# A post-norm attention and expert layer on one core: three waits moved at once

## The chip, the core and the metric

One core of one Trainium2 chip runs the whole layer as one program. Its engines are TensorE (PE, matmuls, with PEld for its weight loads), VectorE (DVE), ScalarE (ACT), GpSimd (POOL) and SyncE (SP, which issues most DMAs). The metric is the device time of one execution in microseconds; the figure compared is the median of several executions.

## The reference, cut to what matters

```
x = layernorm(x + attention(x))        # 4 x 512 tokens, 512 wide, 16 heads of 32
x = layernorm(x + top1_expert_ffn(x))  # 4 experts, 512 -> 2048 -> 512

attention: q, k, v = x @ W + b, split into heads
  s = q k^T / sqrt(32) - slope[head] * (T - 1 - key)     # a bias by key position
  s = where(key <= query, s, -huge);  out = softmax(s) v;  return out @ Wo + bo
ffn: logits = x @ Wr + br, the best expert of each token, silu(x Wg) * (x Wu) @ Wd, times its probability
```

All is fp32. The kernel splits operands into a rounded high part and a low part and adds three products (high*high, low*high, high*low) for each fp32 product.

## The kernel before

The program has two stages. The first is attention over 4 batches of 16 heads; the second gathers the rows of each expert and runs the feed-forward part. The change lies in the first stage alone.

**Steps.** Attention is a pipeline of steps. A head has three units (n = 0, 1, 2: some of its query or key tiles), so 64 heads give units 0 to 191, and step u does the following for units of different age. TensorE runs `unit_scores(u)` (queries by keys), `unit_turned(u - 7)` (the same scores with keys on the partitions), once a head `row_of_maxima` (turning the row maxima), then a slice of side work, `unit_values(u - 10)` (weights by values), once a head `head_values`, and a second slice of side work. VectorE runs `unit_biased(u)` (adds the bias to the scores in place and takes the minimum of the negated sum: the row maximum, line 1290) and `unit_masked(u - 7)` (adds the causal mask to the turned scores, line 1307). ScalarE then runs `unit_exp(u - 7)` (line 1035), and `unit_split` (the high part of the weights) a step later; GpSimd makes the low part one step behind (`unit_low`, line 1627).

**End of a head.** When a head's last unit of values is done, ScalarE copies the sum out of its PSUM bank at the end of its step (`head_copied`, line 1048, tile pvT, in steps with u = 0 modulo 3, behind `unit_exp` of that step). TensorE turns that copy in the next step (`head_values`, line 837, four transposes, u = 1 modulo 3), waiting on the semaphore s_pvT. ScalarE and VectorE read the turned result one step later (lines 1055, 1315, 1316), GpSimd scales it (line 1621).

**Side work.** The projections (jobs K, Q, V of a group of four heads, 12 matmuls of 512 columns or 24 of 256), the transposes of x, the output projection OP with its transposes OT, the layernormed row's transposes x1t and the gate's logits are cut into single matmuls. A planner (`make_plan`) lays them into two halves of each step, `plan.slices[u, 0]` ahead of the values and `plan.slices[u, 1]` behind them, by a queue, a budget for each half step and due times. A finished job is taken over at the start of the next step by ScalarE (high part, `take`) and then VectorE (low part, `take`), both ahead of their units. When the queue is empty, or no job in it is ready, a step has no side work. The plan can be worked out from the code alone: steps 12 to 20 (group 1) hold V for the second half of the first batch's keys, then K and Q of group 2, and steps 21 to 23 hold nothing.

**Order on an engine.** Each engine works strictly in the order in which the code issues. In step u VectorE's order is: take-overs, layernorm moments, layernorm, `unit_biased(u)`, `unit_masked(u - 7)`, `head_values`.

**The stacks.** The scores of a head need its q and k parts laid below each other on 96 partitions (tile stack, six slots). DMAs issued by SyncE put them there. For the first four heads this happens right after the first K and Q: heads 0 and 1 first K, then Q, then heads 2 and 3, six small DMAs for a head (line 563). Later heads get three DMAs each (line 579). ScalarE may overwrite q and k with the next group's K only when all stacks of the group before have landed (line 991 and the waits above it).

Of the kernel before, what the change touches and what calls it, by code (L numbers as in the profile page):

```python
# [110 lines left out]
def is_head_step(u, lag):  # L111

    return u >= lag and (u - lag) % PER_HEAD == 0 and (u - lag) // PER_HEAD < NB * NH
# [50 lines left out]
def make_plan():  # L164
# [76 lines left out]
    for u in range(STEPS):  # L241
        flush(u)
        if u in SPLIT_BY:
            ready.add(("split", SPLIT_BY[u]))
        if later:
            kind, t = later.popleft()
            if kind == "moments":
                plan.moments_at[u] = t
            else:
                plan.normal_at[u] = t  # L250
                fresh.append(("ln", t))
        for t in range(2 * QT, NT):
            if plan.flushed.get(("OP", t - 2 * QT), STEPS) + X_LOAD <= u:
                ready.add(("x", t // QT, t % QT))
        if u < WORK:
            g = min(u // PER_GROUP, NG - 1)
            step = u - g * PER_GROUP
            b, m = divmod(g, GPB)
            if step == 0:

                if g == 0:
                    queue.extend([("K", 1), ("Q", 1), ("bv_wo", 0)])
                elif m == 0:
                    queue.appendleft(("V", g // 2, 1))
                    rows_due.extend((b - 1, n) for n in range(QT + 3))
                elif g == 1:
                    queue.append(("V", 1, 0))
                elif m == 1 or g == 2:
                    queue.appendleft(("V", b * GPB // 2 + 1, 1))
                for _ in range(row_counts[b == LAST][m] if b else 0):  # L270
                    queue.extend(row_jobs(*rows_due.popleft()))
                if m == GPB - 1 and b + 1 < NB:
                    next_x = b + 1
                    queue.append(("V", (g + 1) // 2, 0))
            for j in range(QT):

                if next_x and ("x", next_x, j) in ready and ("xT", next_x, j) not in turned:
                    turned.append(("xT", next_x, j))
                    queue.appendleft(turned[-1])
            if m == 0 and g and step == VL:  # L280
                queue.append(("V", g // 2 + 1, 0))
            if step == KQ_STEP and 0 < g < NG - 1:
                if m == 2 and 0 < b < LAST:
                    queue.extend([("K", g + 1), ("Q", g + 1)])
                else:
                    first = [j for j in queue if j[0] == "xT" or m == 0 and j[0] == "V"]
                    for j in first:
                        queue.remove(j)
                    queue.extendleft(reversed(first + [("K", g + 1), ("Q", g + 1)]))
            if u == U:  # L290
                for t in range(T0, NT):
                    if t > T0:
                        queue.append(("OP", t - 1))
                    queue.append(("OT", t))
                queue.append(("OP", NT - 1))
            work(u, 0, budget(u, 0))
        if is_head_step(u, VL + PER_HEAD + 2):
            ready.add(("o", (u - VL - PER_HEAD - 2) // PER_HEAD))

        if u >= U:  # L300
            ready.update(fresh)
        if u < WORK:
            work(u, 1, budget(u, 1))
        ready.update(fresh)
        fresh.clear()
# [18 lines left out]
def build(nc, x, Wq, bq, Wk, bk, Wv, bv, Wo, bo, Wr, br, Wg, Wu, Wd,  # L324
# [7 lines left out]
    with ExitStack() as ctx:  # L332
# [178 lines left out]
        kqv_done = max(done("K", NG - 1), done("Q", NG - 1), done("V", NG // 2 - 1, 1))  # L511

        def stack_count(hd):
            return 16 * (3 * (hd // NSTK + 1) + (3 if hd % NSTK < GH else 0))

        def x1T_at(t):
            return t % 2 if t >= T0 else 0
# [24 lines left out]
        hot_f = hot_pad[:, NT - 1:2 * NT - 1, :].bitcast(F32)  # L542
        ends, begins, count = route[:, TILES, 0, :], route[:, TILES, 1, :], route[:, TMP, 0, :]
        number, found = banks[2][:, 0:NS], route[:, POS, :, :].rearrange("p t e -> p (t e)")[:, 0:NS]


        def sync(sp):
# [18 lines left out]
            def load_first_stack(h, n, job):  # L566
                sp.wait_ge(s_side_act, plan.act_number[job])
                load_first_part(h, n, False)
                sp.wait_ge(s_side_dve, plan.number[job])
                load_first_part(h, n, True)  # L570

            def load_stacks(hd):

                g, h = divmod(hd, GH)
                sp.wait_ge(s_side_dve, max(done("K", g), done("Q", g)))
                if hd >= NSTK:
                    sp.wait_ge(s_sT, (hd - NSTK + 1) * PER_HEAD)
                for r, (q_part, k_part) in enumerate(STACKED):
                    sp.dma_start(stack[r * HD:(r + 1) * HD, hd % NSTK, :, :].bitcast(F32),
                                 qk[h * HD:(h + 1) * HD, q_part:k_part + 1:k_part - q_part, :].bitcast(F32)  # L580
                                 ).then_inc(s_stack[hd % NSTK], 16)

            def load_row(hd):

# [47 lines left out]
            for h in (0, 1):  # L632
                load_first_stack(h, WK, ("K", 0))
            for h in (0, 1):
                load_first_stack(h, WQ, ("Q", 0))
            for h in (2, 3):
                load_first_stack(h, WK, ("K", 0))
                load_first_stack(h, WQ, ("Q", 0))
            next_stack = GH
            for u in range(STEPS):  # L640
# [36 lines left out]
        def tensor(pe):  # L677
# [155 lines left out]
            def head_values(hd):  # L833
                bank = banks[4 + hd % 2]
                pe.wait_ge(s_pvT, hd + 1)
                for i in range(QT):
                    mm = pe.transpose(bank[:, i * VW:(i + 1) * VW], pvT[:, i * P:(i + 1) * P], ident[0:VW, 0:VW])
                mm.then_inc(s_back, 1)
# [3 lines left out]
            for u in range(STEPS):  # L842
                if u < U:
                    unit_scores(u)
                if LAG <= u < U + LAG:
                    unit_turned(u - LAG)
                if is_head_step(u, ROW_AT):
                    row_of_maxima((u - ROW_AT) // PER_HEAD)
                if u < WORK:
                    for job, i0, i1 in plan.slices[u, 0]:  # L850
                        side(job, i0, i1)
                if u >= VL:
                    unit_values(u - VL)
                if is_head_step(u, VL + PER_HEAD):
                    head_values((u - VL - PER_HEAD) // PER_HEAD)
                if u < WORK:
                    for job, i0, i1 in plan.slices[u, 1]:
                        side(job, i0, i1)
            head_values(NB * NH - 1)
            for job in plan.after_loop + plan.tail:  # L860
                side(job, 0, len(cost_of(job)))
# [100 lines left out]
        def scalar(act):  # L962
            def split_weight(n, part):
                cols = columns(n, part)
                if n == WQ:
                    act.wait_ge(s_wq, part + 1)
                else:
                    act.wait_ge(s_w[n, part], 16)
                act.activation(w_hi[n][:, :, cols], w_raw[:, n, :, cols], ACT.Copy).then_inc(s_whi, 1)
# [110 lines left out]
            take(("Q", 0))  # L1080
            split_weight(WK, 1)
            split_weight(WQ, 1)
            take(("V", 0, 0))
            take(("V", 0, 1))
            split_weight(WV, 1)
# [128 lines left out]
        def vector(dve):  # L1214
# [61 lines left out]
            def normalise(t):  # L1276
                dve.wait_ge(s_rstd, t + 1)
                dve.tensor_scalar(x1_row(t), x1_row(t), mv[:, t % 2, 0:1], rstd[:, t % 2, 1:2],
                                  ALU.subtract, ALU.mult).then_inc(s_ln, 1)
# [30 lines left out]
            def head_values(hd):  # L1310
                parts = banks[4 + hd % 2][:, 0:QT * VW].rearrange("p (i d) -> p i d", i=QT)
                dve.wait_ge(s_pvhi, hd + 1)
                if hd >= 2:
                    dve.wait_ge(s_o, hd - 1)
                dve.reciprocal(row_inv[:, hd % 2, :], pv_hi[:, hd % 2, :, HD]).then_inc(s_inv, 1)
                dve.tensor_tensor(pv_sum[:, hd % 2, :, :], parts[:, :, HD + 1:VW], pv_hi[:, hd % 2, :, 0:HD],
                                  ALU.add).then_inc(s_pvsum, 1)
# [11 lines left out]
            for u in range(STEPS):  # L1329
                for job in plan.taken_at[u]:  # L1330
                    take(job)
                if u in plan.moments_at:
                    moments(plan.moments_at[u])
                if u in plan.normal_at:
                    normalise(plan.normal_at[u])
                if u < U:
                    unit_biased(u)
                if LAG <= u < U + LAG:
                    unit_masked(u - LAG)
                if is_head_step(u, VL + PER_HEAD + 1):  # L1340
                    head_values((u - VL - PER_HEAD - 1) // PER_HEAD)
            head_values(NB * NH - 1)
# [426 lines left out]
```

## Time and profile before

| | before |
|---|---|
| median of 2 executions | 1288.54 us (1288.02 to 1289.06) |
| profiled execution: time, span | 1292.03 us, 1290.2 us |
| TensorE busy over the span | 1169.2 us (91%) |
| VectorE, ScalarE, GpSimd busy | 729.2 us (57%), 588.6 us (46%), 521.6 us (40%) |
| granted TensorE clock, mean | 0.947 of full |

Every number below is from the one profiled execution. A span runs from the first instruction to the last. The granted clock is a share of 2.4 GHz: 1.00 is the full level and 0.50 the lower one of 1.2 GHz. In the timeline the bracket at the end of a row is the time for which the engine stood idle before it and what ended that. The attention stage runs from the start to about 530 us, the feed-forward stage from about 565 us.

### The profile page before, as it was taken

The numbers are of one execution on the slowest core, as the hardware profiler recorded it, in microseconds if no ns is written. First come the engines' busy times: TensorE is split into PE (matmuls) and PEld (weight loads), VectorE is DVE, ScalarE is ACT, GpSimd is POOL, SyncE is SP. The second block draws the span as 40 slices with busy tenths as digits, with TensorE's granted clock in tenths as the row PEclk, the third lists the DMA queues.
The fourth block names the chain that finished last, engine by engine and source line by source line (L and its number), as shares of the span: only waits on it lengthen the run. The fifth ranks groups of instructions, "written<-read, shape, count | busy, mean of one in ns | idle before, by whom it ended". The sixth has DMA issues, their size and how long they took to land.

```text
span 1290.2 us, 25813 instructions
## 1 busy us (share of the span) xinstructions
PE 1169.2 (91%) x7658; PEld 1040.4 (81%) x7658; DVE 729.2 (57%) x1975; ACT 588.6 (46%) x1475; POOL 521.6 (40%) x662
## 2 busy tenths in 40 slices
PE   7888888998898888669999999999999999999994
PEld 5677777777787676559988998899889988998993
DVE  4555556556655564456565456645664566366565
ACT  3577765676576557424232323332333233233344
POOL 6855644565455456453133123302330232033236
PEclk9898998999889887769999999999999999999997
DMA  8223323222322232144212231223122313231302
GB/s 271 56 50 71 67 74 84 58 62 65 88 55 58 58 77 63 51 124 129 83 58 74 72 94 53 80 66 99 50 83 67 99 50 83 67 99 42 91 26 106
DMA packets 105534, 100.10 MB, mean 78 GB/s; under 512 B 10367, under 2 KB 79615, under 8 KB 105408
## 3 DMA queue, kind: packets, MB, share of 16 engines
q1 hardware_dynamic: 100640, 87.97, 25.4%
q0 software_dynamic: 3040, 9.18, 2.2%
q8 instruction: 75, 1.23, 0.4%
q10 hardware_dynamic: 1728, 1.31, 0.3%
q14 instruction: 51, 0.42, 0.1%
HBM read 64.74 MB, written 9.18 MB: 57 GB/s over the span
## 4 chain that ended last, share of the span: by engine, by line
PE 48%; POOL 6%; DMA 3%; issue 3%; ACT 2%; DVE 2%; SPq 0%; ACTq 0%; POOLq 0%; DVEq 0%
PE bank L910 34%; PE bank L935 8%; POOL up_lo L1636 5%; PE bank L922 2%; DMA up_raw<-in_Wu_dram 2%; PE bank L682 1%; ACT up_hi L1065 1%; PE bank L776 1%; PE bank L884 1%; POOL out_dram L1703 1%; ACT probs L1035 0%; DVE bank L1290 0%; DMA y<-x_scratch,row_token 0%; PE bank L828 0%; PE bank L872 0%
## 5 line engine op out<-in xcount | busy, mean ns | idle before, releaser
L1636 POOL TENSOR_TENSOR up_lo<-up_raw,up_hi 128x256 fp32r<-128x256 f32 x241 | 171.6, 747 | 480.8 <-ACT up_hi L1065 480.6
L910 PE MATMUL bank<-up_hi,xsT_hi 128*128 x1216 | 356.2, 293 | 8.4 <-POOL up_lo L1636 6.6
L910 PE MATMUL bank<-up_hi,xsT_lo 128*128 x1216 | 344.6, 283 | 0.0
L910 PE MATMUL bank<-up_lo,xsT_hi 128*128 x1216 | 344.5, 283 | 0.0
L1627 POOL TENSOR_TENSOR pT_lo<-probs,pT_hi 128x512 fp32r<-128x512 f32 (+1 forms) x192 | 210.7, 1103 | 188.4 <-ACT pT_hi L1042 187.8
L1451 DVE SCALAR_TENSOR_TENSOR h_tok<-bank,row_weight,silu 128x128 f32<-128x128 f32 x304 | 93.4, 347 | 294.7 <-ACT silu L1145 294.7
L910 PEld LDWEIGHTS bank<-up_hi,xsT_hi 128*128 128x128 f32 x1216 | 233.3, 192 | 15.1 <-issue 14.9
L910 PEld LDWEIGHTS bank<-up_hi,xsT_lo 128*128 128x128 f32 x1216 | 234.0, 192 | 0.3
L910 PEld LDWEIGHTS bank<-up_lo,xsT_hi 128*128 128x128 f32 x1216 | 233.6, 192 | 0.0
L1145 ACT ACTIVATE silu<-bank 128x256 f32<-128x256 f32 (+1 forms) x160 | 59.9, 374 | 367.5 <-PE bank L910 367.5
L1468 DVE TENSOR_TENSOR y<-bank,y 128x512 f32<-128x512 f32 x295 | 199.0, 689 | 0.5
L1035 ACT ACTIVATE probs<-bank,key_bias 128x256 f32<-128x256 f32 (+3 forms) x256 | 126.4, 519 | 109.0 <-DVE bank L1307 109.0
L1290 DVE CUSTOM_DVE_ANT_0 bank<-bank,dist 128x512 f32<-128x512 f32 (+3 forms) x256 | 123.2, 503 | 78.5 <-PE bank L788 78.0
L935 PE MATMUL bank<-down_hi,hT_hi 128*128 x304 | 124.2, 408 | 1.3 <-DVE y L1468 0.6
L1065 ACT ACTIVATE up_hi<-up_raw 128x256 fp32r<-128x256 f32 x256 | 85.3, 408 | 83.5 <-DMA up_raw<-in_Wu_dram 83.5
L935 PE MATMUL bank<-down_lo,hT_hi 128*128 x304 | 119.1, 392 | 0.0
L935 PE MATMUL bank<-down_hi,hT_lo 128*128 x304 | 119.0, 392 | 0.0
L1042 ACT ACTIVATE pT_hi<-probs 128x512 fp32r<-128x512 f32 (+1 forms) x192 | 106.8, 556 | 2.3
L828 PE MATMUL bank<-pT_hi,v 128*65 128x256 f32 (+2 forms) x320 | 86.0, 303 | 1.6 <-POOL pT_lo L1627 1.6
L788 PE MATMUL bank<-stack 96*128 96x512 f32 (+3 forms) x256 | 82.7, 365 | 4.3 <-DVE neg_max L1290 4.1
L828 PE MATMUL bank<-pT_lo,v 128*65 128x256 f32 (+3 forms) x256 | 76.7, 325 | 0.0
L803 PE MATMUL bank<-stack 97*128 97x256 f32 (+3 forms) x256 | 74.6, 333 | 1.1 <-ACT probs L1035 0.9
(181 smaller groups left out, 2096.8 us busy)
## 6 DMA issues: line engine op xcount, KB each, us to landing
stack<-qk SPq DMA_DIRECT2D x180, 128.0 KB, 2.4
up_raw<-in_Wg_dram SPq DMA_DIRECT2D x64, 256.0 KB, 3.1
up_raw<-in_Wu_dram SPq DMA_DIRECT2D x64, 256.0 KB, 3.8
down_raw<-in_Wd_dram SPq DMA_DIRECT2D x64, 256.0 KB, 2.6
x_tok<-in_x_dram SPq DMA_DIRECT2D x16, 256.0 KB, 4.4
x_scratch<-res SPq DMA_DIRECT2D x12, 256.0 KB, 2.2
stack<-qk SPq DMA_DIRECT2D x24, 64.0 KB, 3.2
w_raw<-in_Wo_dram SPq DMA_DIRECT2D x1, 1024.0 KB, 8.8
```

The costliest lines, as they stand in the source:

```text
L788: mm = pe.matmul(bank[:, at:at + width], q_stack[0:3 * HD, slot, i * P:(i + 1) * P], k_stack[0:3 * HD, slot, 0:width], start=True, stop=True)
L828: mm = pe.matmul(bank[0:VW, c0:c1], v[:, g // 2 % 2, j, g % 2 * GH + h, :], part[:, u % NP, at + c0 - j * P:at + c1 - j * P], start=(j == ...
L910: mm = pe.matmul(bank[:, n * 2 * P:(n + 1) * 2 * P], a[:, s, k, :], up_w[w][k][:, :, :].rearrange("p a f -> p (a f)")[:, bass.ds(at, 2 * P ...
L935: mm = pe.matmul(bank[:, :], a[:, s, :], down_w[w][:, :, :].rearrange("p a f -> p (a f)")[:, bass.ds(at, D)], start=(q == 0), stop=(q == 2))
L1035: ex = act.activation(probs[:, u % NP, at:at + width], banks[2 + u % 2][:, at:at + width], ACT.Exp, scale=SLOPE[hd % NH], bias=key_bias[:, ...
L1042: act.activation(pT_hi[:, u % NP, 0:n], probs[:, u % NP, 0:n], ACT.Copy).then_inc(s_pThi, 1)
L1065: act.activation(up_w[0][k][:, e, :], up_raw[:, idx % NUPS, k, :, :].rearrange("p g f -> p (g f)"), ACT.Copy).then_inc(s_uphi, 1)
L1290: bi = dve.tensor_tensor_reduce(out=banks[u % 2][:, at:at + width], in0=banks[u % 2][:, at:at + width], in1=dist[:, SEQ - width:SEQ], scal ...
L1451: hh = dve.scalar_tensor_tensor(h_tok[:, idx % 2, n, :], gu[:, n, 1, :], row_weight[:, s:s + 1], silu[:, idx % 2, n, :], ALU.mult, ALU.mult)
L1468: dve.tensor_tensor(y[:, s, :], banks[D_BANKS[idx % 3]][:, :], y[:, s, :], ALU.add).then_inc(s_y, 1)
L1627: pool.tensor_tensor(pT_lo[:, u % NP, 0:n], probs[:, u % NP, 0:n], pT_hi[:, u % NP, 0:n].bitcast(F32), ALU.subtract).then_inc(s_pTlo, 1)
L1636: pool.tensor_tensor(up_w[1][k][:, e, :], up_raw[:, idx % NUPS, k, :, :].rearrange("p g f -> p (g f)"), up_w[0][k][:, e, :].bitcast(F32), ...
```

## The change

Four edits, all in the attention stage.

1. TensorE issues `head_values` as the last thing of its step, behind the second slice of side work, not ahead of it.
2. VectorE issues `unit_masked(u - 7)` ahead of `unit_biased(u)`.
3. The stacks of heads 2 and 3 are issued by ScalarE, three whole DMAs for each head, after the first K and Q are through VectorE; SyncE issues those of heads 0 and 1 only. The counts waited for follow.
4. In group 1 (steps 12 to 23) the planner queues the job V of the next two groups behind K and Q, at the third step; before, it was queued at the first step and ran ahead of them.

```
-                elif g == 1:
-                    queue.append(("V", 1, 0))
-                elif m == 1 or g == 2:
+                elif m == 1 and b or g == 2:
                     queue.appendleft(("V", b * GPB // 2 + 1, 1))
...
             if step == KQ_STEP and 0 < g < NG - 1:
-                if m == 2 and 0 < b < LAST:
+                if g == 1:
+                    queue.extend([("K", 2), ("Q", 2), ("V", 1, 0)])
+                elif m == 2 and 0 < b < LAST:
...
-            return 16 * (3 * (hd // NSTK + 1) + (3 if hd % NSTK < GH else 0))
+            return 16 * (3 * (hd // NSTK + 1) + (3 if hd % NSTK < GH // 2 else 0))
...
             for h in (0, 1):
-                load_first_stack(h, WQ, ("Q", 0))
-            for h in (2, 3):
-                load_first_stack(h, WK, ("K", 0))
                 load_first_stack(h, WQ, ("Q", 0))
...
                 if u >= VL:
                     unit_values(u - VL)
-                if is_head_step(u, VL + PER_HEAD):
-                    head_values((u - VL - PER_HEAD) // PER_HEAD)
                 if u < WORK:
                     for job, i0, i1 in plan.slices[u, 1]:
                         side(job, i0, i1)
+                if is_head_step(u, VL + PER_HEAD):
+                    head_values((u - VL - PER_HEAD) // PER_HEAD)
...
             split_weight(WQ, 1)
+            act.wait_ge(s_side_dve, done("Q", 0))
+            for h in (2, 3):
+                for r, (q_part, k_part) in enumerate(STACKED):
+                    act.dma_start(stack[r * HD:(r + 1) * HD, h, :, :].bitcast(F32),
+                                  stack_rows(h, q_part, k_part)).then_inc(s_stack[h], 16)
             take(("V", 0, 0))
...
+                if LAG <= u < U + LAG:
+                    unit_masked(u - LAG)
                 if u < U:
                     unit_biased(u)
-                if LAG <= u < U + LAG:
-                    unit_masked(u - LAG)
```

## Rows read from the trace of the kernel before

**Rows 1.** Waits of TensorE over the span: engine, line, releaser: us, times, longest

```profile
PE bank L837 <- ACT pvT L1048: 42.6, 38, 2.8
```

**Rows 2.** Timeline of steps 100 to 103: start us, us, engine, line, operation

```profile
264.85 0.46 PE L837 MATMUL bank<-ident,pvT 65*128 65x65 f32 x4 [0.64 <-ACT pvT L1048]
...
266.07 0.40 PE L682 MATMUL bank<-xT_lo,w_hi 128*128 128x512 f32 x1
...
266.31 0.39 PE L682 MATMUL bank<-xT_hi,w_hi 128*128 128x512 f32 x1
...
267.68 0.69 ACT L991 ACTIVATE qk<-bank,bias_col 128x512 fp32r<-128x512 f32 x1
...
268.40 0.75 DVE L1235 SCALAR_TENSOR_TENSOR qk<-bank,bias_col,qk 128x512 fp32r<-128x512 f32 x1 [1.29 <-ACT qk L991]
...
269.06 0.69 DVE L1290 CUSTOM_DVE_ANT_0 bank<-bank,dist 128x512 f32<-128x512 f32 x1
...
269.67 0.47 DVE L1307 TENSOR_TENSOR bank<-bank,causal 128x256 f32<-128x256 f32 x1
...
270.17 0.84 ACT L1035 ACTIVATE probs<-bank,key_bias 128x384 f32<-128x384 f32 x2 [1.29 <-DVE bank L1307]
...
270.90 0.59 ACT L1048 ACTIVATE pvT<-bank 65x512 f32<-65x512 f32 x1
...
271.54 0.46 PE L837 MATMUL bank<-ident,pvT 65*128 65x65 f32 x4 [0.77 <-ACT pvT L1048]
271.81 0.48 PE L682 MATMUL bank<-xT_hi,w_hi 128*128 128x512 f32 x1
```

**Rows 3.** Timeline of TensorE, line 837, two heads with side work

```profile
59.20 0.46 PE L837 MATMUL bank<-ident,pvT 65*128 65x65 f32 x4 [0.61 <-ACT pvT L1048]
...
432.25 0.46 PE L837 MATMUL bank<-ident,pvT 65*128 65x65 f32 x4 [0.88 <-ACT pvT L1048]
```

**Rows 4.** Timeline of TensorE, line 837, a head with a V job beside it

```profile
152.87 0.46 PE L837 MATMUL bank<-ident,pvT 65*128 65x65 f32 x4 [1.52 <-ACT pvT L1048]
```

**Rows 5.** Timeline of TensorE, line 837, heads beside the output projection, and one more wait

```profile
192.55 0.46 PE L837 MATMUL bank<-ident,pvT 65*128 65x65 f32 x4 [1.79 <-ACT pvT L1048]
...
201.75 0.46 PE L837 MATMUL bank<-ident,pvT 65*128 65x65 f32 x4 [1.17 <-ACT pvT L1048]
...
202.96 0.50 PE L682 MATMUL bank<-xT_hi,w_hi 128*128 128x512 f32 x1 [0.30 <-DVE oT_lo L1247]
```

**Rows 6.** Timeline of TensorE, line 837, heads without side work

```profile
72.56 0.46 PE L837 MATMUL bank<-ident,pvT 65*128 65x65 f32 x4 [2.21 <-ACT pvT L1048]
...
346.47 0.46 PE L837 MATMUL bank<-ident,pvT 65*128 65x65 f32 x4 [2.83 <-ACT pvT L1048]
```

**Rows 7.** Timeline of TensorE, line 837, the last head

```profile
523.11 0.47 PE L837 MATMUL bank<-ident,pvT 65*128 65x65 f32 x4 [0.68 <-ACT pvT L1048]
```

**Rows 8.** Busy us in two stretches: stretch, length, PE, PEld, DVE, ACT, POOL, PEclk, DMA, GB/s

```profile
266.00:273.00 7.00, 6.23 (x37) 4.97 (x36) 3.89 (x15) 5.21 (x13) 3.94 (x5) 1.00 0.00 0
...
75.00:77.50 2.50, 2.50 (x13) 2.31 (x13) 0.62 (x3) 2.30 (x5) 1.73 (x3) 0.50 0.51 116
```

**Rows 9.** Timeline of the start, engine by engine (SPq is a DMA issue)

```profile
17.63 16.31 SPq L563 DMA_DIRECT2D stack<-qk  x24
...
20.22 2.85 ACT L969 ACTIVATE w_hi<-w_raw 128x1536 fp32r<-128x1536 f32 x2
24.46 0.61 ACT L996 ACTIVATE v<-bank 128x512 fp32r<-128x512 f32 x1 [1.39 <-PE bank L682]
...
35.46 0.69 ACT L991 ACTIVATE qk<-bank,bias_col 128x512 fp32r<-128x512 f32 x1 [6.57 <-DMA stack<-qk]
...
37.72 0.76 PE L788 MATMUL bank<-stack 96*128 96x512 f32 x1 [3.43 <-DVE neg_max L1290]
...
39.23 0.30 POOL L1585 TENSOR_SCALAR causal<-causal 128x128 f32<-128x128 f32 x1
...
41.64 0.77 PE L788 MATMUL bank<-stack 96*128 96x512 f32 x1 [0.70 <-DVE neg_max L1290]
```

More of the change, by code:

```diff
@@ L544, in build, with stack_rows @@
         number, found = banks[2][:, 0:NS], route[:, POS, :, :].rearrange("p t e -> p (t e)")[:, 0:NS]
+        def stack_rows(h, q_part, k_part):
+            return qk[h * HD:(h + 1) * HD, q_part:k_part + 1:k_part - q_part, :].bitcast(F32)
         def sync(sp):
@@ L579, in load_stacks @@
                     sp.dma_start(stack[r * HD:(r + 1) * HD, hd % NSTK, :, :].bitcast(F32),
-                                 qk[h * HD:(h + 1) * HD, q_part:k_part + 1:k_part - q_part, :].bitcast(F32)
-                                 ).then_inc(s_stack[hd % NSTK], 16)
+                                 stack_rows(h, q_part, k_part)).then_inc(s_stack[hd % NSTK], 16)
             def load_row(hd):
```

## The prediction, made before the change was run

> **What bounds the kernel now.** I read the waits of TensorE first, since it is busy for 91% of the span and whatever it waits for is lost. One line leads the list by far: the four transposes that turn a head's values wait 42.6 us, in 38 of the 64 heads, for ScalarE's copy of these values [rows 1]. I then followed that wait through the timeline of every head, to see which chain is late and what TensorE could have done meanwhile. Last came the start and the windows of the granted clock. The feed-forward stage is untouched and only starts earlier.
>
> One head shows the chain [rows 2]. At step 102 ScalarE takes over a finished Q at 267.68, VectorE its low part at 268.40, then VectorE takes the minimum of step 102 from 269.06, then adds the mask at 269.67; the exponential follows at 270.17, the copy behind it at 270.90, and TensorE, already in step 103, goes on at 271.54 after 0.77 us of idle time. The matmuls right behind the transposes (271.81) are side work that needs none of this. So the wait holds up work that was ready, and the chain that ends it carries a minimum that nobody on the chain needs.
>
> **Edit 1, the transposes behind the second slice.** TensorE now does that slice while the copy is made. Two matmuls of 512 columns are the usual slice; they start 0.24 us apart at the full clock (266.07 and 266.31 [rows 2]), so it hides 0.48 us; three hide 0.72 us, and so do six V matmuls of 256 columns, at half the price each. What is queued behind the transposes is the next step's scores; who waits for them is ScalarE, one step later, ahead of its exponential. That exponential waits for turned scores of that later step in any case, which TensorE issues behind these transposes, so I cost the later arrival at nothing. If ScalarE were not about a step behind, it would cost up to the slice, 0.48 us a head.
>
> **Edit 2, the mask first.** The mask moves up by the spacing of the two VectorE instructions, 269.67 - 269.06 = 0.61 us, and so do the exponential and the copy [rows 2]. VectorE now waits for the turned scores before it takes the minimum: the minimum ends about as late as the mask is long, 0.47 us, plus the wait for one more group of matmuls where VectorE is early. Behind it hang the scores two steps on. The minimum would end at 269.06 + 0.47 + 0.69 = 270.2, 2.5 us after the take-over at 267.68, near the start of its step; a head takes 271.54 - 264.85 = 6.7 us now [rows 2], about 6.0 without the wait, and two of its three steps 4.0 us. So more than a microsecond is to spare, and I cost it at nothing; the third rival is the case that this is wrong.
>
> **The 38 waits, by what lies beside them.** They add up as follows, each read from its own row of the timeline, with the plan of side work beside it.
> - 18 heads with an ordinary slice in the second half, 0.16 to 0.88 us, 10.9 us together (the first and last: 0.61 and 0.88) [rows 3]. Slice and mask give 0.48 + 0.61 = 1.09 us, more than any of them. Gain 10.9 us.
> - 3 heads with six V matmuls in both halves, 1.52, 1.51 and 1.51 us, of which one stands [rows 4]. 0.72 + 0.61 = 1.33, and the slice of the first half also runs ahead of the wait. I take 1.4 each: 4.2 us.
> - 4 heads beside the output projection, 1.79, 1.80, 1.97 and 2.57 us (the first stands [rows 5]). Three matmuls and the mask: 0.72 + 0.61 = 1.3 each, 5.2 us.
> - 2 heads with a transpose and K matmuls in the second half, 1.17 and 1.16 us. Here the slice itself waits on VectorE, 0.30 us for oT_lo right after [rows 5], and that comes from the same chain. Only the mask's 0.61 helps: 1.2 us.
> - 5 heads with no side work in the second half, 2.22, 1.77, 2.81, 1.77 and 2.83 us (the last stands [rows 6]). Edit 1 moves nothing there; the mask gives 0.61 each, 3.1 us.
> - 1 head in group 1, 2.21 us [rows 6], is edit 4, below.
> - 5 late heads, 0.27, 1.10, 0.59, 0.45 and 0.68 us (the last stands [rows 7]). The last two come when there is no minimum left, so nothing changes; 1.4 us of the others.
>
> Sum without the group-1 head: 10.9 + 4.2 + 5.2 + 1.2 + 3.1 + 1.4 = 26.0 us.
>
> **Edit 4, V behind K and Q in group 1.** By the code, K and Q run in steps 14 to 19 instead of 15 to 20 and V in steps 20 to 23, three matmuls a half, instead of steps 12 to 14. That fills the head that waits 2.21 us [rows 6], and empties steps 12 and 13, where the first head did not wait. The same chain then shows there. Bounds are 2.2 us either way; I take a gain of 1.5 us, since the first head's copy is done before TensorE would be much early.
>
> **Edit 3, the first stacks.** SyncE needs 16.31 us for 24 issues, 0.68 us each, so the last stack lands after 34 us, and ScalarE can take over K of the next group only at 35.46, after waiting 6.57 us; that holds VectorE, and TensorE idles 3.43 us for a minimum [rows 9]. With ScalarE's six issues behind its weight splits, which end at 23.07, they would be out at 23.07 + 6 x 0.68 = 27.2 us, and the wait is gone. Their own price: the take-over of the first V moves from 24.46 to 27.2, the second one and the first minimum by some 0.3 us; all later queues but ScalarE's are free of it.
>
> The 3.43 us do not come back whole. The mask itself is made by GpSimd and ends at 39.53 [rows 9], with a weight split ahead of it that moves 0.3 us later with ScalarE: 39.8. With edit 2, VectorE stands at its first mask until then, and the minimum queued behind holds the scores that now start at 41.64 to about 39.8 + 0.4 + 0.7 = 40.9 or a little more. Lower bound 0, upper bound 3.4; I take 1.4, close to the GpSimd row.
>
> The Trainium skill (DMA: Bandwidth & Descriptors, Issuing engines are not separate DMA queues) speaks against such an edit: DMAs from whichever engine end up on the same 16 DMA engines, and its rules for authors add that spreading saves only the sequencer's issue time. Here it is issue time that the row shows, so by that rule too the wait would go; if transfers were the limit instead, the start would give 0 in place of 1.4 us.
>
> **What comes back.** TensorE at full clock arrives earlier at its other waits, above all those for a take-over by VectorE, such as 0.30 us for oT_lo [rows 5]. I price this at one such wait for each of the 27 heads that lose most of theirs, 27 x 0.3 = 8 us; bounds 0 and 16. The room is thin but there: in a 7 us stretch at the full clock ScalarE is busy 5.21 and GpSimd 3.94 us [rows 8], which is 5.0 and 3.8 us of a head of 6.7 us that would become one of 6.0.
>
> **The clock.** Between 70 and 500 us, 43 windows of 2.5 us show a granted clock below 1.00, some of them at 0.50 throughout, as at 75 to 77.5, behind the 2.21 us idle of the group-1 head [rows 6, 8]. A matmul takes twice as long in them. They add to some 68 us at 1.2 GHz. Seven of the stretches follow a wait that I expect to lose more than half of itself; by their windows they hold 24 us, worth 12 us if TensorE were the only limit at full clock. Other engines then wait less too, and the emptied steps 12 and 13 may bring one more. Bounds -3 and 12; I take 3.
>
> **The sum.** 26.0 + 1.5 + 1.4 + 3 - 8 = 24 us less. The profiled execution, 1292.0 us with 1.8 us around its span, would be 1268; the median, 3.5 us below it, goes from 1288.5 to 1264.
>
> **Rivals.**
> - The wait moves on. TensorE is held by ScalarE's and VectorE's own loop: take-over, mask, exponential. For: ScalarE is busy 5.21 of 7 us and stands in series with VectorE at each take-over (1.29 us idle [rows 2]). Against: with the mask first the idle time falls to 1.29 - 0.61 = 0.7 us, and 5.0 us of work and 0.7 of idle time fit into a head of 6.0. If it decides, some half of the 28.9 us stays: 1274.
> - The clock pays more. The Trainium skill (TensorE: Matmul & The Clock Gate, Part 1) has it that activity lifts the throttle, so filled gaps would keep the full level. As a mechanism of this kernel: all seven stretches behind shortened waits go, 12 us instead of 3, and the come-back is small: 1250.
> - The minimum becomes the bound. VectorE waits for the turned scores, then masks, and only then frees the score bank; from the point where two steps of TensorE are shorter than those 2.5 us, which steps without side work can be, the scores wait. At 0.9 us (the mask's 0.47 and the wait for one matmul group) for each of 64 heads it costs 58 us against 29 gained: 1317, slower.
> - The change doesn't do what it says: the next step's scores or exponentials wait for what the transposes waited for, and the 42.6 us only change their line: 1288.
>
> **How the numbers follow.** Forecast 0.50, wait moves on 0.27, clock 0.13, no effect 0.06, minimum 0.04. Two per cent, about what a measurement of this kernel can tell from no change, is 25.8 us: below 1262.8. The forecast's terms leave it on that side in about half of its cases, and the clock case lies there: 0.25 + 0.13 = 0.38 faster; slower 0.03 (the minimum case, where it costs that much), within 2% 0.59. The range goes from the clock case, 1250, to the second case with its upper come-back, 1281.
>
> **What the profile after would show.** The wait for pvT at the transposes should fall from 42.6 to about 15 us, left in heads without side work (about 1.6 to 2.2 us each). The mask should stand ahead of the minimum by some 0.6 us, and the idle time of ScalarE ahead of that exponential should shrink from 1.29 to about 0.7 us. ScalarE's 6.57 us wait for stacks should be gone, and the first mask should start when GpSimd's mask is ready, near 39.8. Stretches at 0.50 should be fewer. I am wrong if a new line of TensorE's waits takes over (scores for a minimum, turned scores for an exponential, values for pT_lo), or if the shortened stalls bring the clock up everywhere.

## The result and the profile after

The changed kernel took 1243.01 us (median of two executions, 1241.00 to 1245.01) against 1288.54: a ratio of 0.9647, with an interval of 0.9578 to 0.9716. That is 45.5 us less, where 24 were forecast, and below the range. The profiled execution took 1245.0 us, with a span of 1243.2.

I read the busy line of the page first (engine, busy us, share, instructions).

```profile
PE 1149.7 (92%) x7658; PEld 1028.2 (83%) x7658; DVE 728.6 (59%) x1975; ACT 589.2 (47%) x1475; POOL 520.8 (42%) x662
```

TensorE carries out the same number of matmuls, but is busy for 1149.7 us instead of 1169.2. Its idle time, span less busy, went from 121.0 to 93.5 us. So the 47.0 us by which the span shrank are two things: 27.5 us of idle time and 19.5 us of matmuls that went faster. The second part is the one that the forecast had nearly left out.

The waits of TensorE over the span (line, releaser: us, times, longest) answer to [rows 1]:

```profile
PE bank L837 <- ACT pvT L1048: 13.6, 17, 1.6
...
PE bank L682 <- DVE oT_lo L1252: 6.0, 9, 1.5
...
PE bank L788 <- DMA stack<-qk: 5.1, 5, 2.1
...
PE bank L788 <- DVE neg_max L1295: 2.6, 3, 1.6
...
PE bank L768 <- DVE logits L1272: 1.6, 2, 0.8
```

The wait for pvT fell from 42.6 to 13.6 us; about 15 was forecast. Two lines have no counterpart before: the scores' wait for their stacks, and a wait for the gate's logits.

The timeline of steps 102 and 103 answers to [rows 2]:

```profile
244.97 0.69 ACT L991 ACTIVATE qk<-bank,bias_col 128x512 fp32r<-128x512 f32 x1 [0.36 <-PE bank L682]
...
245.69 0.75 DVE L1240 SCALAR_TENSOR_TENSOR qk<-bank,bias_col,qk 128x512 fp32r<-128x512 f32 x1 [1.08 <-ACT qk L991]
...
246.36 0.42 DVE L1312 TENSOR_TENSOR bank<-bank,causal 128x256 f32<-128x256 f32 x1
...
246.69 0.69 DVE L1295 CUSTOM_DVE_ANT_0 bank<-bank,dist 128x512 f32<-128x512 f32 x1
...
246.82 0.84 ACT L1035 ACTIVATE probs<-bank,key_bias 128x384 f32<-128x384 f32 x2 [0.64 <-DVE bank L1312]
...
247.55 0.59 ACT L1048 ACTIVATE pvT<-bank 65x512 f32<-65x512 f32 x1
...
247.89 0.39 PE L682 MATMUL bank<-xT_hi,w_hi 128*128 128x512 f32 x1
...
248.12 0.39 PE L682 MATMUL bank<-xT_hi,w_lo 128*128 128x512 f32 x1
...
248.35 0.41 PE L837 MATMUL bank<-ident,pvT 65*128 65x65 f32 x4
```

Read it against the chain of before. The mask (246.36) stands ahead of the minimum (246.69). ScalarE waits 0.64 us ahead of its exponential, not 1.29. The copy ends at 248.14, and TensorE spends that time on two matmuls of the slice (247.89, 248.12); the transposes follow at 248.35 without a wait. The minimum is finished 2.4 us after the take-over began (247.38 - 244.97; 2.5 was forecast), and no scores wait for it here.

Other heads keep or lose their wait as their side work has it:

```profile
50.12 0.46 PE L837 MATMUL bank<-ident,pvT 65*128 65x65 f32 x4 [0.80 <-ACT pvT L1048]
...
89.60 0.46 PE L837 MATMUL bank<-ident,pvT 65*128 65x65 f32 x4 [1.56 <-ACT pvT L1048]
...
139.22 0.46 PE L837 MATMUL bank<-ident,pvT 65*128 65x65 f32 x4 [0.16 <-ACT pvT L1048]
...
175.08 0.46 PE L837 MATMUL bank<-ident,pvT 65*128 65x65 f32 x4 [0.40 <-ACT pvT L1048]
...
472.73 0.70 PE L837 MATMUL bank<-ident,pvT 65*128 65x65 f32 x4 [0.68 <-ACT pvT L1048]
```

In this order: the first head, which now waits because edit 4 emptied its steps; a head without side work, 1.56 instead of 2.22 us; a V head, 0.16 instead of 1.52 [rows 4]; a head beside the output projection, 0.40 instead of 1.79 [rows 5]; the last head, unchanged [rows 7].

The start answers to [rows 9] (SPq and ACTq are DMA issues):

```profile
17.96 7.90 SPq L567 DMA_DIRECT2D stack<-qk  x12
...
22.29 3.27 ACTq L1086 DMA_DIRECT2D stack<-qk  x5
...
25.61 0.61 ACT L996 ACTIVATE v<-bank 128x512 fp32r<-128x512 f32 x1 [2.16 <-issue]
...
29.25 0.50 PE L788 MATMUL bank<-stack 96*128 96x512 f32 x1 [2.08 <-DMA stack<-qk]
...
34.77 0.69 ACT L991 ACTIVATE qk<-bank,bias_col 128x512 fp32r<-128x512 f32 x1 [6.02 <-PE bank L682]
...
39.43 0.30 POOL L1590 TENSOR_SCALAR causal<-causal 128x128 f32<-128x128 f32 x1
...
39.87 0.30 DVE L1312 TENSOR_TENSOR bank<-bank,causal 128x128 f32<-128x128 f32 x1
...
40.95 0.77 PE L788 MATMUL bank<-stack 96*128 96x512 f32 x1 [1.63 <-DVE neg_max L1295]
```

ScalarE's next K is no longer held by a stack but by TensorE, and begins at 34.77 instead of 35.46. The first mask starts at 39.87, right behind GpSimd's (39.43 + 0.30), and the scores behind it at 40.95 (40.9 was forecast). So these scores start 0.69 us earlier than before. The price stands at 29.25: the first scores wait 2.08 us for their own stack.

The list of DMA issues (issuer, number, KB each, median us from issue to landing) shows the stacks of the first heads. Before, all 24, then the first 12 and the last 12 of them:

```profile
stack<-qk SPq DMA_DIRECT2D x24, 64.0 KB, 3.2
...
stack<-qk SPq DMA_DIRECT2D x12, 64.0 KB, 5.3
...
stack<-qk SPq DMA_DIRECT2D x12, 64.0 KB, 2.1
```

After:

```profile
stack<-qk SPq DMA_DIRECT2D x12, 64.0 KB, 5.8
...
stack<-qk ACTq DMA_DIRECT2D x6, 128.0 KB, 5.8
```

The 5.8 us of SyncE's twelve must be held against the 5.3 of the same twelve before; the 3.2 is low because the last twelve landed in 2.1 us. So ScalarE's DMAs beside them went with landings about half a microsecond later.

The clock at one place. Columns as in [rows 8]; the same 2.5 us stood at 0.50 before, with 13 matmuls (the work in this window is not the same in the two kernels, so only the clock compares):

```profile
75.00:77.50 2.50, 2.50 (x17) 2.10 (x16) 1.73 (x5) 1.91 (x5) 1.37 (x2) 1.00 0.59 129
```

**The account used below.** For each kernel I cut the first 600 us of the profiled execution into stretches of 2.5 us and added up, from their granted clock, the time at the lower level: (1 - clock) x 2 x 2.5 us each. Of it 37.5 us lie in the routing between the two stages in every kernel, 41.0 in one (mask first alone).

| kernel | span | TensorE busy | idle | wait for pvT | at the lower level |
|---|---|---|---|---|---|
| before | 1290.2 | 1169.2 | 121.0 | 42.6 | 122.9 |
| after | 1243.2 | 1149.7 | 93.5 | 13.6 | 81.8 |
| e1_turn | 1272.6 | 1160.2 | 112.4 | 26.5 | 99.1 |
| e2_mask | 1247.6 | 1151.7 | 95.9 | 21.9 | 88.7 |
| e12_turn_mask | 1250.0 | 1156.0 | 94.0 | 13.7 | 102.5 |
| b_fill2 | 1274.0 | 1171.0 | 103.0 | 25.9 | 78.5 |
| m_copy | 1267.5 | 1164.4 | 103.1 | 23.3 | 109.4 |
| m_other | 1272.3 | 1158.9 | 113.4 | 40.2 | 98.9 |
| a_fill2 | 1232.8 | 1150.2 | 82.6 | 5.0 | 58.0 |
| e3_stacks | 1286.4 | 1163.7 | 122.7 | 43.7 | 109.2 |
| e4_plan | 1280.0 | 1163.5 | 116.5 | 42.5 | 105.8 |

One execution is not the median. The last column changes between executions: the mean granted clock of the five executions of e12_turn_mask runs from 0.954 to 0.962, which is 21 us at the lower level over their spans, and the profiled one is the slowest. So the column is read for its trend, and the medians decide.

### The profile page after: what moved, and what is told of

The parts are those of the page before. It is cut to its first block, busy times and chain, and to the rows that moved or that the text cites. A ratio compares the mean times of both kernels' runs of the same rounds, so it can differ in the third digit from the quotient of the medians.

```text
span 1243.2 us, 25807 instructions
## 1 busy us (share of the span) xinstructions
PE 1149.7 (92%) x7658; PEld 1028.2 (83%) x7658; DVE 728.6 (59%) x1975; ACT 589.2 (47%) x1475; POOL 520.8 (42%) x662
## 4 chain that ended last, share of the span: by engine, by line
PE 50%; POOL 7%; DMA 3%; issue 2%; ACT 2%; DVE 1%; SPq 0%; ACTq 0%; POOLq 0%; DVEq 0%
PE bank L910 36%; PE bank L935 8%; POOL up_lo L1641 5%; DMA up_raw<-in_Wu_dram 3%; PE bank L922 3%; PE bank L682 1%; ACT up_hi L1065 1%; PE bank L776 1%; PE bank L884 1%; POOL out_dram L1708 1%; POOL pT_lo L1632 0%; DMA y<-x_scratch,row_token 0%; PE bank L872 0%; ACT pT_hi L1042 0%; ACT probs L1035 0%
## 5 line engine op out<-in xcount | busy, mean ns | idle before, releaser
L1312 DVE TENSOR_TENSOR bank<-bank,causal 128x128 f32<-128x128 f32 (+1 forms) x192 | 65.4, 341 | 68.8 <-PE bank L803 46.9
L828 PE MATMUL bank<-pT_hi,v 128*65 128x256 f32 (+2 forms) x320 | 83.4, 294 | 1.4 <-POOL pT_lo L1632 1.3
L935 PEld LDWEIGHTS bank<-down_hi,hT_hi 128*128 128x128 f32 x304 | 57.0, 187 | 22.9 <-issue 10.1
```

The lines of the kernel that those rows point to most:

```text
L828: mm = pe.matmul(bank[0:VW, c0:c1], v[:, g // 2 % 2, j, g % 2 * GH + h, :], part[:, u % NP, at + c0 - j * P:at + c1 - j * P], start=(j == ...
L935: mm = pe.matmul(bank[:, :], a[:, s, :], down_w[w][:, :, :].rearrange("p a f -> p (a f)")[:, bass.ds(at, D)], start=(q == 0), stop=(q == 2))
```

## The experiments

Each was timed against the kernel before on the same chip; medians, range and number of executions are given, and the ratio with its interval.

**Edits 1 and 2, each alone and together.** e1_turn moves only the call of `head_values` on TensorE behind the second slice. e2_mask moves only `unit_masked(u - LAG)` ahead of `unit_biased(u)`. e12_turn_mask has both and the old stacks and plan.

> Only the transposes moved behind the second slice of side work. Theory C (the waits go, and the clock then stays up longer): the wait for the copy falls by what the slice covers, about 14 us, and some 6 us more come from fewer stretches at the lower clock: about 1268. Rival W (the waits alone count, the clock is a bystander): 1275. Rival M (the mask order is what matters, the place of the transposes little): above 1282.

> Only the mask ahead of the minimum on VectorE. Theory C: the wait for the copy falls by up to 0.61 us in each of some 33 heads, about 19 us, and the clock adds some 7: about 1262. Rival W: 1269. Rival T (the place of the transposes is what matters): above 1280.

> Both orders changed, stacks and plan as before. Theory C: nearly all of the gain, 1248 to 1253, with stretches at the lower clock far shorter than before between 70 and 500 us (68 us before, 44 us with the whole change). Rival S (the start and the plan of group 1 bring what the prediction missed): 1262 or above.

| kernel | median | range, executions | ratio |
|---|---|---|---|
| e1_turn | 1273.78 | 1265.61 to 1274.40, 4 | 0.9839 [0.9798, 0.9880] |
| e2_mask | 1248.86 | 1247.19 to 1250.42, 4 | 0.9665 [0.9638, 0.9692] |
| e12_turn_mask | 1242.96 | 1241.09 to 1251.80, 5 | 0.9616 [0.9590, 0.9643] |

Against 1290.75 for the kernel before beside them they are worth 17, 42 and 48 us: the mask alone brings most, the turn adds 6 to it, and the pair alone is as fast as the whole change. The expectations missed: e1_turn came out near the 1275 of waits that count alone rather than at the 1268 with the clock, and the other two below what was expected. The two do not add up since they pay for the same waits. Waits of TensorE in e1_turn:

```profile
PE bank L837 <- ACT pvT L1048: 26.5, 25, 2.8
PE bank L682 <- DVE oT_lo L1247: 8.4, 12, 1.6
...
PE bank L706 <- DVE xT_lo L1231: 3.7, 3, 1.5
```

and in e2_mask:

```profile
PE bank L837 <- ACT pvT L1048: 21.9, 20, 1.9
...
PE bank L682 <- DVE oT_lo L1247: 4.8, 10, 1.5
```

In e1_turn the pvT wait falls by 16.1 us but the idle time by only 8.6. Of the 7.5 us between, 6.0 stand on lines of VectorE's chain: oT_lo 8.4 us (before 5.9), xT_lo 3.7 (before 1.9), logits 1.7 (before none). In e2_mask pvT falls by 20.7 us and the idle time by 25.1: nothing comes back, more goes. Hiding a wait behind work leaves the chain as late as it was, and TensorE meets part of it again elsewhere; shortening the chain makes everything behind it earlier.

The sizes per head fit the prediction. In e1_turn, line 837:

```profile
71.55 0.70 PE L837 MATMUL bank<-ident,pvT 65*128 65x65 f32 x4 [2.21 <-ACT pvT L1048]
...
148.65 0.47 PE L837 MATMUL bank<-ident,pvT 65*128 65x65 f32 x4 [0.81 <-ACT pvT L1048]
...
264.50 0.46 PE L837 MATMUL bank<-ident,pvT 65*128 65x65 f32 x4 [0.32 <-ACT pvT L1048]
```

The head without a slice keeps its 2.21 us [rows 6]; six V matmuls take 1.52 to 0.81, 0.71 us (0.72 forecast); an ordinary slice takes 0.77 [rows 2] to 0.32, 0.45 us (0.48 forecast).

**Useless work in the old gaps.** If the busy time that vanished is the clock, then filling the idle time with matmuls that nobody needs should win time as well, with no chain any shorter. Into the kernel before I put 3 to 9 such matmuls of 512 columns ahead of the transposes in heads that wait more than 1 us, on a side bank that was already taken over. They add work and leave none out.

```
+            def idle(n, u):
...
+                    pe.wait_ge(s_side_dve, plan.number[job])
...
+                    for _ in range(n):
+                        pe.matmul(side_banks[b][:, :], w_hi[WO][:, 0, 0:P], w_hi[WO][:, 0, :], start=True, stop=True)
...
+                idle(END.get(u, 0), u)
                 if is_head_step(u, VL + PER_HEAD):
                     head_values((u - VL - PER_HEAD) // PER_HEAD)
```

b_fill does it in 16 heads:

> The kernel before, with 3 to 9 matmuls of no use (512 columns, into a side bank whose job is done) ahead of the transposes in the 16 heads that wait longest, some 0.8 of each wait long at the full clock. No wait is removed and no order changed. Theory C: TensorE stays at the full level through these stretches, and the time falls by 8 to 17 us, to 1272 to 1281. Rival W: 1288 or a little more, since the same chain ends each wait.

It took 1287.52 us (1284.46 to 1292.07, 10 executions), 0.9976 [0.9953, 0.9998]: hardly a difference, and the number of the rival. But it tells little by itself, because of its own flaw:

```profile
188.14 2.06 PE L850 MATMUL bank<-w_hi 128*128 128x512 f32 x6 [3.00 <-DVE x1T_lo L1282]
```

In three heads (steps 73, 121 and 181) the filler itself waited for its bank, 3.0 to 3.8 us each, 9.8 us together. b_fill2 leaves these three out and has 76 useless matmuls in 13 heads.

> As the run with matmuls of no use ahead of the transposes, without the three heads in which these matmuls themselves stood for x1T_lo (3.0, 3.0 and 3.8 us). No wait is removed. If a higher clock is worth half a us for each us no longer at the lower level, whatever else waits: some 30 us fewer, about 1275. If the waits take back what the clock gives (the chain to the copy does not get shorter): 1281 to 1287.

It took 1276.93 us (1274.98 to 1278.73, 4 executions), 0.9889 [0.9863, 0.9916] against 1291.19. At the 0.23 us by which matmuls of this width follow each other at the full clock (247.89 and 248.12 above), the fillers are 17.5 us of work, and the idle time fell by 18.0. Swapped one for one, that alone would change nothing. The 14 us gained are the clock: busy time rose by 1.8 instead of 17.5 us, and the mean granted clock was 0.962 to 0.967 in the four executions, against 0.947 to 0.954 in the seven of the kernel before beside them. At the group-1 head [rows 6, 8] the waits and the same window show it:

```profile
72.61 0.47 PE L856 MATMUL bank<-ident,pvT 65*128 65x65 f32 x4 [0.60 <-ACT pvT L1068]
```

```profile
75.00:77.50 2.50, 2.50 (x25) 2.40 (x23) 1.59 (x8) 2.35 (x5) 1.79 (x3) 1.00 0.56 123
```

Seven fillers leave 0.60 us of the 2.21 us wait, and behind it TensorE runs at the full level, 25 matmuls in the time of 13.

**This head in all kernels** is a test of its own. A stretch at the lower level begins between 70 and 75 us in each of the seven kernels in which this head waits 1.5 us or more (before, e1_turn, e2_mask, e12_turn_mask, m_copy, m_other, e3_stacks; waits of 1.55 to 2.21 us), and in none of the seven in which it waits 0.60 us or less (after twice, b_fill, b_fill2, e4_plan, a_fill2 twice). The next long wait, four heads later, is less clear-cut: there a stretch follows in eight of the ten profiles with a wait of 1.56 to 2.22 us (not in m_other and e4_plan), and in none of the four with 0.25 to 0.47 us. So a wait of this size is often followed by the lower level, not always.

**Which steps need the mask first.** m_copy puts the mask ahead of the minimum only in the steps in which ScalarE makes the copy; m_other only in the other two of three (`!= 0` in the first line).

```
+                first = u % PER_HEAD == 0
+                if first and LAG <= u < U + LAG:
+                    unit_masked(u - LAG)
                 if u < U:
                     unit_biased(u)
-                if LAG <= u < U + LAG:
+                if not first and LAG <= u < U + LAG:
                     unit_masked(u - LAG)
```

> Of the kernel before, the mask ahead of the minimum only in the steps at whose end the copy of a head's values is made (one step in three). Theory (only the chain to the copy counts): as with the mask first in every step, 1249, within 4 us. Rival (the exponential and the weights come earlier in every step): at most half of the gain, 1270 or above.

> The counterpart: the mask ahead of the minimum only in the other two steps of three. Theory (only the chain to the copy counts): little, 1283 to 1290. Rival: 1265 or below.

m_copy: 1264.26 us (1257.88 to 1269.28, 4 executions), 0.9772 [0.9733, 0.9812]. m_other: 1277.01 us (1274.06 to 1280.38, 4 executions), 0.9896 [0.9870, 0.9922]. That is 27 and 14 us, together about the 42 of e2_mask; both came out between theory and rival. Waits for pvT in m_copy:

```profile
PE bank L837 <- ACT pvT L1048: 23.3, 20, 2.1
```

and in m_other:

```profile
PE bank L837 <- ACT pvT L1048: 40.2, 36, 2.6
```

The wait for pvT belongs to the step of the copy, as I had it: m_copy takes away 19.3 of the 20.7 us that e2_mask does, m_other 2.4. But the time does not follow that wait alone, as the theory of both had it. m_other loses 7.6 us of idle time, spread over several lines, and 10.3 us of busy time, with 24 us less at the lower level. Why the full level lasts longer there, when its pvT waits are nearly all left, these runs don't settle.

**Edits 3 and 4 alone.** e3_stacks has only the stacks of heads 2 and 3 on ScalarE, e4_plan only V behind K and Q in group 1.

> Only the stacks of heads 2 and 3 moved to ScalarE's queue. The 6.57 us wait of ScalarE for stacks and the 3.43 us of TensorE at the start should go; the steps behind still run into GpSimd's mask and weight split. Theory: 1 to 3 us at the first head, and whatever the clock makes of the rest: 1284 to 1292, no more than the spread of the kernel before. Rival (the start is worth as much as the waits): 1280 or below.

> Only the plan of group 1 changed. The wait of 2.21 us in the head without side work goes, one of up to 2 us appears at the first head. Theory: 1286 to 1292, no difference. Rival (filled steps keep the clock up in the heads behind): 1283 or below, with the stretch at the lower level at 74 to 78 us gone.

e3_stacks: 1289.54 us (1283.53 to 1294.39, 10 executions), 1.0003 [0.9977, 1.0028]. e4_plan: 1286.74 us (1281.33 to 1293.23, 10 executions), 0.9983 [0.9955, 1.0011]. Neither can be told from no change, as expected. In e3_stacks the timeline of TensorE at the start shows why:

```profile
38.71 0.47 PE L788 MATMUL bank<-stack 96*128 96x512 f32 x1 [1.25 <-DVE neg_max L1295]
...
42.29 0.80 PE L803 MATMUL bank<-stack 97*128 97x384 f32 x2 [3.11 <-ACT probs L1035]
```

The 3.43 us wait for a minimum [rows 9] became one of 1.25, but TensorE then waits 3.11 us for the first exponentials, which wait for GpSimd's mask (it ends at 40.99 there, 39.53 before). e4_plan cuts the wait at the group-1 head to 0.47 us and removes the lower level behind it, but the first head then waits 1.41 us and a lower-level stretch of 3.4 us comes at 150.

**After, with its own gaps filled.** a_fill2 is the changed kernel with 2 to 5 useless matmuls at the end of 14 steps in which TensorE still stands idle, ahead of the transposes where the step has them (52 in all); after_again is the changed kernel once more, timed beside it.

> The changed kernel with 2 to 5 such matmuls in 14 steps in which TensorE still idles. With most waits gone, TensorE is the limit, so each us brought back to the full level should give half a us: if half of the 44 us (70 to 500 us) come back, about 1233. Rival (the chain of the other engines is the limit): 1243 or more.

> The changed kernel once more, beside the one with matmuls of no use, on one chip: 1241 to 1246.

> The changed kernel with matmuls of no use in 14 idle steps, beside the changed kernel. If TensorE is the limit there and the clock is what such steps cost: 4 to 9 us below the changed kernel. Rival: within 2 us of it.

| kernel | median | range, executions | ratio |
|---|---|---|---|
| a_fill2 | 1239.40 | 1234.55 to 1242.05, 4 | 0.9603 [0.9574, 0.9632] |
| after_again | 1243.80 | 1238.87 to 1245.76, 6 | 0.9638 [0.9604, 0.9673] |
| a_fill2_again | 1238.96 | 1235.26 to 1242.24, 6 | 0.9615 [0.9581, 0.9649] |

Its pvT wait:

```profile
PE bank L856 <- ACT pvT L1068: 5.0, 13, 1.1
```

The median of a_fill2_again is 4.8 us below after_again on the same chip, within the 4 to 9 expected; a_fill2 lay between its two cases, 1233 and 1243. In the profiles idle time falls by 10.9 us and busy time stays (1150.2 against 1149.7) in spite of 12 us of added work; but the profiled a_fill2 is the fastest of its four executions and that of after the slower of two, so these profiles overstate it. It is the fastest kernel here, by a margin that its range doesn't fully clear.

## Why the prediction missed

The direction and the mechanism held; two terms of the sum were mis-sized, both in the same direction. The forecast was 24 us, the profiled executions differ by 47.0. Of the 23 us between, 16.5 are busy time and 6.5 the come-back.

**The waits: right in total.** 27.5 us were forecast for the 38 waits with edit 4 (26.0 + 1.5); the line fell by 29.0. The hiding (0.45 us for a slice), the mask's 0.61 (2.22 to 1.56 us in a head without side work, 0.66) and their sum held for most heads. All 18 waits of 0.16 to 0.88 us are gone. That the total fits so well is in part luck, for some classes missed both ways. The two heads with K matmuls, 1.17 us, which I gave only the mask's 0.61, lost their pvT wait entirely, and by edit 1, not by the mask (none left in e1_turn, 1.26 us in e2_mask); but logits and oT_lo then held TensorE 0.79 and 1.02 us in the same steps. Two heads without side work lost 1.25 and 1.27 us, twice the mask's 0.61, and the late heads 0.2 us net instead of 1.4, since one that had not waited now waits 1.12 us.

**"The clock ... I take 3": the step that failed.** Busy time fell by 19.5 us for the same 7658 matmuls, beyond the upper bound of 12. I had counted only the seven stretches behind waits that lose more than half, and discounted their 12 us to 3. Those seven did go: all in after_again (81.9 us at the lower level by the account) and six in after, where the seventh step keeps one for another reason, below. They hold 24 us; the other 17 lie in stretches that I hadn't counted. By the account, 41.1 us less were spent at the lower level, where a matmul takes twice as long: half of that, 20.5 us, is the busy time that should go. The Trainium skill (TensorE: Matmul & The Clock Gate, HAM oscillation — how this bites in real kernels) works out the penalty in this way, as throttled time times one less the clock's share, and the trace agrees, 20.5 against 19.5. In the other comparisons with before that add no matmuls, between a third and two thirds of the change came out as busy time (m_copy 4.8 of 13.5, e1_turn 9.0 of 23.8, e2_mask 17.5 of 34.2, e12_turn_mask 13.2 of 20.4).

The waits that are left still cost clock. In after, a stretch still begins behind the head at 89.60, which waits 1.56 us, and two begin at 184 and 300, right behind the waits for logits and oT_lo named above (the second in the step of one of the seven; the rows are of the first):

```profile
182.50 0.66 PE L768 MATMUL bank<-ident,res 128*128 128x128 f32 x4 [0.79 <-DVE logits L1272]
...
184.18 0.70 PE L682 MATMUL bank<-xT_hi,w_hi 128*128 128x512 f32 x1 [1.02 <-DVE oT_lo L1252]
```

That the matmuls themselves are no faster shows where both kernels run at the full level. From one V head to the next four heads take, before and after:

```profile
252.32:278.24 25.92, 22.83 (x157) 19.52 (x154) 14.73 (x59) 19.26 (x45) 19.47 (x20) 1.00 0.22 48
```

```profile
231.23:253.90 22.67, 22.51 (x159) 19.94 (x157) 14.77 (x58) 18.41 (x43) 18.64 (x20) 1.00 0.21 46
```

At 1.00 in both, the stretch shrinks by 3.25 us, of which 2.92 are the four waits (3.08 to 0.16) and 0.32 busy time, some 0.1 us for a removed wait (a matmul behind a wait is drawn a little longer). For 21 fewer waits that is 2 us. So about 17 of the 19.5 us are the clock in this pair of executions. The mean granted clocks of many executions agree: 0.961 in the median of after_again, over a span of 1242 us, against 0.950 over 1287 in the 23 of the kernel before beside it. By the formula of the account that is 97 and 129 us at the lower level, and half of the difference is 16 us. That the clock follows the filled gaps, and not the shorter chain, is shown by b_fill2 and by the group-1 head.

**"What comes back", 8 us: too much.** Idle time fell by 27.5 us where the pvT line lost 29.0, so 1.5 us net came back, although the stacks' line alone is 5.1 us. e1_turn shows that the come-back exists: up to 7.5 us there (16.1 - 8.6). I had priced it as if both edits only hid the wait. The mask first makes what ScalarE and VectorE owe TensorE earlier, and takes the come-back away.

**Edits 3 and 4: 2.9 us forecast, none measured.** e12_turn_mask without them has the time of after (1242.96 against 1243.01 and 1243.80). The mask made by GpSimd did take over, at 39.87 as forecast. What I had not costed is that the first scores wait for their own stack: 2.08 us in after, 3.88 in after_again. That edit 3 causes this is not shown: e3_stacks, with the same stacks, has 0.19 us, and of the nine kernels with the old stacks eight have 0 to 1.39 and m_other 2.15. Edit 4's 1.4 us of pvT wait (2.21 to 0.80) is in the 29.0, but no median shows it.

**The rivals.** "The clock pays more" is what happened, with its stretches gone and a small come-back, at 1243 instead of 1250, since other stretches went too. "The wait moves on" is what edit 1 does by itself, and edit 2 cancels. "The minimum becomes the bound" did not occur: the scores' wait for the minimum is 2.6 us in all, before 4.1. "No effect" fell with the pvT line.

## What to carry to other kernels

Where a wait ends a chain, shorten the chain first: taking an instruction that nobody on it needs off its middle was worth 42 us, hiding the wait behind ready work 17, and only the first left nothing to come back. Price a TensorE stall of a microsecond or two at more than its length when the granted clock falls behind such stalls, by the lower-level time in the whole stage rather than at the stalls that one expects to remove. A few useless matmuls in the gaps measure that price directly, and where a gap can't be closed they can pay by themselves, if their bank is surely free.

## What the hardware showed that I had not expected

Work that nobody needs made the kernel faster: 76 matmuls in 13 gaps of the kernel before took 14 us off its median. No chain became shorter by them; the clock rose.

Moving DMA issues from SyncE to ScalarE's queue freed the issuer (12 issues in 7.90 us instead of 24 in 16.31 [rows 9]), and ScalarE's six larger ones were issued at 0.65 us each, partly beside its weight splits. But SyncE's twelve landed no sooner for it: 5.8 us after their issue, in e3_stacks with nothing else changed 6.1 us (5.8 to 6.8 in the five profiles with these stacks), where the same twelve took 5.3 us before (5.0 to 5.7 in the nine with the old stacks). The Trainium skill (DMA: Bandwidth & Descriptors, Issuing engines are not separate DMA queues) says that DMAs interleave on the same 16 engines whoever starts them. The trace agrees in so far as the DMAs of both queues took equally long (5.8 and 5.8 us, of 64 and 128 KB); which of their packets shared an engine these rows don't show.
